# Three flags in place of one for the weights' low parts in a macaron transformer block

## The chip, the cores and the metric

The kernel runs on one core of a Trainium2 chip. The metric is the device time of one execution in microseconds, from the first instruction to the last with what lies around them; smaller is better. TensorE is called PE here, VectorE DVE, ScalarE ACT, GpSimd POOL and the engine that issues the transfers SP.

## The reference

The input is x of 16 x 256 tokens with 128 features. Three residual steps follow one another: half a feed-forward network, a 16-head self-attention, and the same half feed-forward network again.

```python
x = x + 0.5 * ffn(layernorm(x));  x = x + attention(layernorm(x));  x = x + 0.5 * ffn(layernorm(x))

def ffn(x):                                   # weights -1, 0 or 1, with a scale per output
    h = silu(tlin(x, w1, s1)) * tlin(x, w2, s2)      # 128 -> 512, twice
    h = gelu(tlin(h, h1, sh1)); h = gelu(tlin(h, h2, sh2))   # 512 -> 512
    return tlin(h, w3, s3)                            # 512 -> 128
```

Everything is float32.

## The kernel before, in words

A float32 product is made of matmuls in a shorter format. Every operand is split into a high part (a copy in that format) and a low part (what is left of it). `split_mm` (line 939) multiplies high weights by the high and the low part of the data. With `general` true it adds the low weights times both parts, which doubles the matmuls. If every low part of the weights is zero, these products add nothing, and the shorter form is exact.

The weights come as eleven chunks of 128 x 512 in seven groups (`W_GROUPS`): group 0 is w1, group 1 is w2, groups 2, 3 and 4 up to chunk 6 hold h1 and the start of h2 (group 2 is one chunk, groups 3 to 6 two each), and groups 5 and 6 hold the rest of h2 and w3. ACT makes the high part of a group (`weight_hi`, line 444), DVE the low parts of groups 0 and 1 (`weight_lo`, line 624), POOL those of groups 2 to 6 (line 387). DVE reduces the low part of each group to its largest magnitude (`weight_lo_max`, line 629), then the seven of them to one (`all_lo_max`), a matmul with a column of ones sums this over the partitions, DVE copies the sum into `flag`, and PE loads the flag into a register (line 1182). `If_ne` on the register (line 1183) then chooses between two written-out versions of the rest of the phase, `ffn_bodies` with `general` true or false. The register also chooses the version in the second feed-forward phase.

The tokens are taken in blocks of 512, two blocks to a pass. A pass is `layer1` (eight tiles t; each a product with w1, the gate, and one with w2, the up), then `hidden` four times (h1 for block 0 and 1, then h2 for block 0 and 1; four tiles of eight matmuls each), and `output`. The first `layer1`, before the flag is known, always takes the general form: 64 matmuls in place of 32. Inside a tile of `layer1`, ACT applies silu and DVE multiplies it by the up product (`silu<-bank,S,silu`); ACT then makes the high part of the result and DVE its low part (`act_lo<-silu,act_hi`). In `hidden`, ACT applies gelu twice and DVE makes the low part (`act_lo<-full,act_hi`).

Nothing plans the order: each engine has its own written list, and semaphores join them. The functions take `between` tables that put extra work behind a tile. PE's list is the one of the functions under `block.tensor`. The gate product of tile t waits for the silu of tile t-3, and the up product for DVE's product of tile t-3. A wait on PE holds all that stands behind it.

Of the kernel before, what the change touches and what calls it, by code (L numbers as in the profile page):

```python
# [56 lines left out]
W_GROUPS = ((0, 1), (1, 2), (2, 3), (3, 5), (5, 7), (7, 9), (9, 11))  # L57
W_RAW = 3


def macaron_kernel(nc, x, w_ffn, w_att, s12, sg, s3, bqk, bv, bo, eye, sel, low_rows, out):
# [11 lines left out]
    with ctx:  # L73
# [31 lines left out]
        newton = sb("newton", [P, 8])  # L105
        lo_max = sb("lo_max", [P, len(W_GROUPS) + 1])
        flag = sb("flag", [1, 1])
        xn = sb("xn", [P, 8, P])
# [330 lines left out]
        def _(act):  # L439
# [61 lines left out]
            def ffn_phase(f):  # L501
# [32 lines left out]
                if f == 0:  # L534
                    weight_hi(0)
                    weight_hi(1)
                    split_x(nb, 0)
                    weight_hi(2)
                    split_x(nb + 1, 1)
                    weight_hi(3)  # L540
                    act.wait_ge(consts_in, 16 * N_CONSTS)
                    layer1(t1, {t: lambda k=t + 4: weight_hi(k) for t in range(3)})
                    act.wait_ge(s3_half, 1)
                else:
                    layer1(t1, {3: lambda: o_to_sbuf(NBATCH - 1)})
# [73 lines left out]
        def _(dve):  # L619
# [16 lines left out]

            def all_lo_max():
# [5 lines left out]
            def take_flag():  # L643
                dve.wait_ge(flag_sum, 1)
                D.tensor_copy(flag[:, :], bank[6][0:1, 0:1]).then_inc(flag_set, 1)

# [143 lines left out]
            def ffn_phase(f):  # L790
                t1, t2, nb, n0 = f * NB * HT, f * NP * HID_TILES, f * NB, f * NORMS1

                def body(i, first=False, more=True):
# [8 lines left out]
                    for step in steps[0:1]:  # L802
                        step()

                    def first_step():
# [35 lines left out]
                if f == 0:  # L841
# [13 lines left out]
                    side = {t: lambda k=t + 2: weight_lo_max(k) for t in range(5)}  # L855
                    layer1(t1, side | {5: all_lo_max, 6: take_flag})

# [77 lines left out]
        def _(pe):  # L935
# [155 lines left out]
            def ffn_bodies(f, general):  # L1091
                t1, t2, nb, nx = f * NB * HT, f * NP * HID_TILES, f * NB, f * XN1

                def body(i, first=False, more=True):
# [3 lines left out]
                    pe.wait_ge(h_full, hl + 6)  # L1098
                    hidden(g, 0, 0, h_lo, hl + HT, general)
                    before = nb + 2 * i - 2  # L1100
# [11 lines left out]
                    hidden(g + HT, 0, 1, h_lo, hl + 2 * HT, general, back | ({3: tokens} if into_att else {}))  # L1112
                    hidden(g + 2 * HT, 1, 0, g_lo, g + HT + SLOTS, general,
# [38 lines left out]
                if f == 1:  # L1152
# [6 lines left out]
                    pe.wait_ge(att_added, NBATCH)  # L1159
                body(0, first=True)  # L1160
                with pe.Fori(1, NP - 1) as i:
# [3 lines left out]
            def ffn_phase(f, low_weights):  # L1165
                if f == 0:
                    pe.wait_ge(eye_in, 16)
                    transpose_x(0, 0)
                    transpose_x(1, 1)

                    pe.wait_ge(w_lo, 2)
                    def sum_low_max():


                        pe.wait_ge(ones_set, 1)
                        pe.wait_ge(lo_reduced, len(W_GROUPS) + 1)
                        MM(bank[6][0:1, 0:1], ONES[:, 0:1], lo_max[:, len(W_GROUPS):len(W_GROUPS) + 1],
                           start=True, stop=True).then_inc(flag_sum, 1)
                    layer1(0, 0, True)
                    sum_low_max()  # L1180
                    pe.wait_ge(flag_set, 1)
                    pe.reg_load(low_weights, flag[0:1, 0:1].bitcast(I32))
# [143 lines left out]
```

## Time and profile before

| | us |
|---|---|
| median of three runs | 709.23 |
| lowest and highest of them | 693.59, 713.70 |
| the profiled execution: its time, its span | 703.42, 701.6 |
| PE busy in the span | 665.2 (95%) |
| DVE, ACT, POOL busy | 459.1, 470.3, 72.4 |

Times in the rows count from the start of the span. A row of the timeline has the start, the duration, the engine, the line, the operation, what it writes and reads, and, in brackets, how long the engine sat idle before it and what ended that. The granted clock of PE (PEclk) is 1.00 at its upper level of 2.4 GHz and 0.50 at 1.2 GHz. What concerns the change lies in the first 60 us of the span.

### The profile page before, as it was taken

The numbers are of one execution on the slowest core, as the hardware profiler recorded it, in microseconds if no ns is written. First come the engines' busy times: TensorE is split into PE (matmuls) and PEld (weight loads), VectorE is DVE, ScalarE is ACT, GpSimd is POOL, SyncE is SP. The second block draws the span as 40 slices with busy tenths as digits, with TensorE's granted clock in tenths as the row PEclk, the third lists the DMA queues.
The fourth block names the chain that finished last, engine by engine and source line by source line (L and its number), as shares of the span: only waits on it lengthen the run. The fifth ranks groups of instructions, "written<-read, shape, count | busy, mean of one in ns | idle before, by whom it ended". The sixth has DMA issues, their size and how long they took to land.

```text
span 701.6 us, 13215 instructions
## 1 busy us (share of the span) xinstructions
PE 665.2 (95%) x4514; PEld 486.0 (69%) x4514; DVE 459.1 (65%) x1067; ACT 470.3 (67%) x786; POOL 72.4 (10%) x240
## 2 busy tenths in 40 slices
PE   2869999999998999999999999999989999999997
PEld 1658888888775656666666666666557887888885
DVE  4845756658548658787878787777218575675742
ACT  2747878879652447676767676766467787886974
POOL 3501010100100102020202020002000101010000
PEclk9989999999995569999999999999589999999999
DMA  8200000000063333242424242400000000100001
GB/s 269 68 2 1 0 1 1 0 0 0 1 240 121 121 116 126 106 137 104 140 100 140 100 139 98 144 1 2 0 3 2 0 1 1 31 1 30 0 30 31
DMA packets 37361, 42.22 MB, mean 60 GB/s; under 512 B 2624, under 2 KB 27968, under 8 KB 37312
## 3 DMA queue, kind: packets, MB, share of 16 engines
q1 hardware_dynamic: 37312, 41.57, 17.4%
q8 instruction: 31, 0.51, 0.3%
q14 instruction: 18, 0.15, 0.1%
HBM read 22.69 MB, written 18.87 MB: 59 GB/s over the span
## 4 chain that ended last, share of the span: by engine, by line
PE 67%; issue 22%; DVE 4%; POOL 3%; ACT 3%; DMA 1%; POOLq 0%; ACTq 0%
PE bank L947 22%; PE bank L1056 11%; PE bank L1031 11%; PE bank L1043 6%; PE bank L1045 5%; PE bank L1074 3%; PE bank L1016 1%; PE bank L1012 1%; PE bank L1088 1%; PE bank L1020 1%; DVE neg_max L758 1%; POOL WL L389 1%; PE bank L1081 1%; POOL newton L366 1%; PE bank L994 1%
## 5 line engine op out<-in xcount | busy, mean ns | idle before, releaser
L947 PE MATMUL bank<-act_hi,WH 128*128 128x512 f32 x576 | 229.3, 398 | 8.0 <-issue 5.1
L947 PE MATMUL bank<-act_lo,WH 128*128 128x512 f32 x576 | 225.3, 391 | 0.0
L758 DVE TENSOR_REDUCE neg_max<-bank 128x2 f32<-128x512 f32 x256 | 169.6, 684 | 61.6 <-PE bank L1031 60.6
L557 ACT ACTIVATE probs<-bank 128x512 f32<-128x512 f32 x256 | 144.6, 597 | 91.7 <-PE bank L1045 90.5
L717 DVE TENSOR_TENSOR act_lo<-full,act_hi 128x512 fp32r<-128x512 f32 x128 | 87.8, 688 | 114.1 <-ACT act_hi L479 113.9
L1043 PE MATMUL bank<-QA,KA 32*128 32x256 f32 x512 | 134.2, 348 | 0.1
L947 PEld LDWEIGHTS bank<-act_hi,WH 128*128 128x128 f32 x576 | 108.7, 189 | 35.0 <-issue 6.4
L477 ACT ACTIVATE full<-bank,SG 128x512 f32<-128x512 f32 x128 | 88.2, 689 | 62.4 <-PE bank L947 62.3
L947 PEld LDWEIGHTS bank<-act_lo,WH 128*128 128x128 f32 x576 | 108.8, 189 | 22.3 <-issue 0.5
L1045 PE MATMUL bank<-m_parts,SEL 32*128 32x256 f32 x512 | 114.2, 290 | 0.0
L1031 PEld LDWEIGHTS bank<-KA,QA 32*128 32x128 f32 x512 | 61.8, 199 | 66.7 <-DVE neg_max L758 46.3
L1031 PE MATMUL bank<-KA,QA 32*128 32x256 f32 x512 | 99.6, 349 | 2.2 <-DVE neg_max L758 1.9
L1043 PEld LDWEIGHTS bank<-QA,KA 32*128 32x128 f32 x512 | 86.2, 197 | 8.3 <-ACT probs L557 5.3
L1056 PE MATMUL bank<-probs,V 128*32 128x256 f32 x1024 | 87.6, 416 | 0.1
L1045 PEld LDWEIGHTS bank<-m_parts,SEL 32*128 32x128 f32 x512 | 87.6, 201 | 0.0
L479 ACT ACTIVATE act_hi<-bank,SG 128x512 fp32r<-128x512 f32 x128 | 87.2, 681 | 0.0
L706 DVE SCALAR_TENSOR_TENSOR silu<-bank,S,silu 128x512 f32<-128x512 f32 x64 | 47.0, 743 | 17.9 <-ACT silu L464 10.5
L947 PE MATMUL bank<-x_hi,WH 128*128 128x512 f32 x128 | 51.9, 406 | 3.7 <-issue 2.9
L947 PE MATMUL bank<-x_lo,WH 128*128 128x512 f32 x128 | 51.3, 401 | 0.0
L464 ACT ACTIVATE silu<-bank,S 128x512 f32<-128x512 f32 x64 | 43.0, 682 | 8.6 <-PE bank L947 8.5
L697 DVE TENSOR_TENSOR act_lo<-silu,act_hi 128x512 fp32r<-128x512 f32 x64 | 45.7, 714 | 0.2
L456 ACT ACTIVATE act_hi<-silu 128x512 fp32r<-128x512 f32 x64 | 40.2, 628 | 6.7 <-DVE silu L706 6.6
(82 smaller groups left out, 571.5 us busy)
## 6 DMA issues: line engine op xcount, KB each, us to landing
qk_scratch<-qk SPq DMA_DIRECT2D x64, 256.0 KB, 2.6
QA<-qk_scratch SPq DMA_DIRECT2D x16, 512.0 KB, 3.8
KA<-qk_scratch SPq DMA_DIRECT2D x16, 512.0 KB, 5.3
X<-x SPq DMA_DIRECT2D x4, 512.0 KB, 9.6
raw_rest<-w_ffn SPq DMA_DIRECT2D x4, 512.0 KB, 6.3
out<-X SPq DMA_DIRECT2D x4, 512.0 KB, 3.2
raw<-w_ffn SPq DMA_DIRECT2D x3, 256.0 KB, 4.3
WA<-w_att SPq DMA_DIRECT2D x1, 256.0 KB, 5.0
```

The costliest lines, as they stand in the source:

```text
L477: A.activation(full[:, t, :], bank[4 + t % 2][:, :], ACT.Gelu, scale=SG[:, layer, t:t + 1])
L479: A.activation(act_hi[1 + layer][:, j, t, :], bank[4 + t % 2][:, :], ACT.Gelu, scale=SG[:, layer, t:t + 1]).then_inc(g_hi, 1)
L557: A.activation(probs[:, v % 8, :], bank[2 + v % 2][:, :], ACT.Exp, scale=SCALE)\
L697: D.tensor_tensor(act_lo[0][:, t // HT, t % HT, :], silu[:, t % SLOTS, :], act_hi[0][:, t // HT, t % HT, :].bitcast(F32), op=ALU.subtract)\
L706: D.scalar_tensor_tensor(out=silu[:, t % SLOTS, :], in0=bank[UP_BANKS[t]][:, :], scalar=S12[:, 1, t % HT:t % HT + 1], in1=silu[:, t % SLOT ...
L717: D.tensor_tensor(act_lo[1 + layer][:, j, t, :], full[:, t, :], act_hi[1 + layer][:, j, t, :].bitcast(F32), op=ALU.subtract)\
L758: D.tensor_reduce(neg_max[:, bb, qt, n0:n0 + 2], bank[A_BANKS[u]][:, :].rearrange("p (h k) -> p h k", h=2), axis=AX.X, op=ALU.max, negate= ...
L947: ins = MM(dst, a, b, start=k == 0, stop=k == len(todo) - 1)
L1031: ins = MM(bank[A_BANKS[u]][:, SEQ * i:SEQ * i + SEQ], QA[rows, 2 * par + bb, 2 * jj + i, P * qt:P * qt + P], KA[rows, 2 * par + bb, 2 * j ...
L1043: MM(dst, KA[rows, 2 * par + bb, 2 * jj + i, P * kt:P * kt + P], QA[rows, 2 * par + bb, 2 * jj + i, :], start=True, stop=False)
L1045: ins = MM(dst, SEL[rows, 2 * jj + i, :], m_parts[rows, bb, :], start=False, stop=True)
L1056: ins = MM(bank[4][32 * h:32 * h + 32, SEQ * (g % 2):SEQ * (g % 2) + SEQ], V[par][:, 2 * bb + kt, col:col + 32], probs[:, (4 * g + 2 * kt ...
```

## The change

Three flags are made instead of one, each over some of the groups: flag 0 over groups 0 and 1 (w1, w2), flag 1 over groups 2 to 4, and flag 2 over all seven. Flag 0 is loaded before anything else on PE, and an `If_ne` on it encloses the transposes of x and the first `layer1`, which now has a general and a short version. Flag 1 is summed behind tile 4 and loaded behind tile 6 of that `layer1`, and an `If_ne` on it encloses the first two calls of `hidden`. Flag 2 is summed inside the second of these calls, behind its tile 2, and loaded behind it; the `If_ne` on it encloses the rest, as the only one did before. ACT converts groups 0 to 4 before it splits x, in place of groups 0 and 1, with 2 and 3 between the halves. DVE reduces groups 0 and 1 and makes flag 0 before it normalises x, reduces group 2 behind that, groups 3 and 4 in `layer1`, and groups 5 and 6 in the second call of `hidden`.

```diff
+FLAGS = ((0, 2), (2, 5), (0, 7))
...
@@ scalar
-                    weight_hi(0)
-                    weight_hi(1)
+                    for k in range(5):
+                        weight_hi(k)
                     split_x(nb, 0)
-                    weight_hi(2)
                     split_x(nb + 1, 1)
-                    weight_hi(3)
                     act.wait_ge(consts_in, 16 * N_CONSTS)
-                    layer1(t1, {t: lambda k=t + 4: weight_hi(k) for t in range(3)})
+                    layer1(t1, {t: lambda k=t + 5: weight_hi(k) for t in range(2)})
                     act.wait_ge(s3_half, 1)
+                    act.wait_ge(w_lo_rest, len(W_GROUPS) - 2)
...
@@ vector
+            def flag_lo_max(f):
                 G = len(W_GROUPS)
-                dve.wait_ge(lo_reduced, G)
-                D.tensor_reduce(lo_max[:, G:G + 1], lo_max[:, 0:G], axis=AX.X, op=ALU.max)\
+                a, b = FLAGS[f]
+                dve.wait_ge(lo_reduced, b + f)
+                D.tensor_reduce(lo_max[:, G + f:G + f + 1], lo_max[:, a:b], axis=AX.X, op=ALU.max)\
                     .then_inc(lo_reduced, 1)
...
+                        third = (lambda: weight_lo_max(5), lambda: weight_lo_max(6), last_flag)
...
-                        hidden(g + HT, 0, 1)
+                        hidden(g + HT, 0, 1, third)
...
                     weight_lo(0)
                     weight_lo(1)
+                    weight_lo_max(0)
+                    weight_lo_max(1)
+                    flag_lo_max(0)
+                    take_flag(0)
                     normalise(n0, 0, 0)
                     normalise(n0, 4, 4)
+                    weight_lo_max(2)
                     low_x(nb, 0)
-                    weight_lo_max(0)
-                    weight_lo_max(1)
                     low_x(nb + 1, 1)
...
-                    layer1(t1, side | {5: all_lo_max, 6: take_flag})
+                    layer1(t1, {1: lambda: weight_lo_max(3), 2: second_flag, 5: lambda: take_flag(1)})
...
@@ tensor
+                        layer1(0, 0, general, {4: second_sum, 6: lambda: load_flag(1)})
+                    def first_hidden(general):
+                        pe.wait_ge(h_full, 6)
+                        hidden(0, 0, 0, h_lo, HT, general)
+                        hidden(HT, 0, 1, h_lo, 2 * HT, general, {2: lambda: sum_low_max(2)})
+                    pe.wait_ge(ones_set, 1)
+                    sum_low_max(0)
+                    load_flag(0)
+                    with pe.If_ne(low_weights, 0):
+                        first_layer1(True)
+                    with pe.Else():
+                        first_layer1(False)
+                    with pe.If_ne(low_weights, 0):
+                        first_hidden(True)
+                    with pe.Else():
+                        first_hidden(False)
+                    load_flag(2)
```

PE, the start of its list in the changed kernel (1188 is the line of the flag's sum, 1009 the transposes of x, 962 the matmuls of `split_mm`). The branch leads to the short version, 71 rows further down, whose first rows stand behind the dots:

```order
L1188 MATMUL bank<-lo_max,ONES 1x1 [waits lo_reduced,ones_set]
L1193 TENSOR_LOAD flag [waits flag_set]
L1213 COMPARE_AND_BRANCH
L1009 MATMUL bank<-EYE,xn 128x128 [waits xn_done,eye_in]
...
L1213 UNCONDITIONAL_BRANCH
L1009 MATMUL bank<-EYE,xn 128x128 [waits xn_done,eye_in]
L1009 MATMUL bank<-EYE,xn 128x128 x3
```

The transposes of x, first in the list before, now stand behind a flag and a branch.

PE in the changed kernel, from the load of flag 1 to the branch on it, and from the sum of flag 2 to the branch on it (both in the short versions):

```order
L1193 TENSOR_LOAD flag [waits flag_set]
L962 MATMUL bank<-x_hi,WH 128x512 [waits silu_done]
...
L962 MATMUL bank<-x_hi,WH 128x512 [waits h_full]
...
L1217 COMPARE_AND_BRANCH
...
L1188 MATMUL bank<-lo_max,ONES 1x1 [waits lo_reduced]
L962 MATMUL bank<-act_hi,WH 128x512 [waits g_hi]
...
L1193 TENSOR_LOAD flag [waits flag_set]
L1222 COMPARE_AND_BRANCH
```

Between the load of flag 1 and its branch stand the four matmuls of tile 7; between the sum of flag 2 and its load the eight of the last tile of `hidden`.

DVE from the low parts of groups 0 and 1 on, in the kernel before and then in the changed one:

```order
L626 TENSOR_TENSOR WL<-raw,WH 128x512 [waits w_hi] x2
L685 TENSOR_SCALAR xn<-X,moments,rstd 128x128 [waits rstd_done]
...
L691 TENSOR_TENSOR x_lo<-bank,x_hi 128x512 [waits xhi_done]
L634 TENSOR_REDUCE lo_max<-WL 128x1 [waits w_lo] x2
L691 TENSOR_TENSOR x_lo<-bank,x_hi 128x512 [waits xhi_done]
```

```order
L626 TENSOR_TENSOR WL<-raw,WH 128x512 [waits w_hi] x2
L634 TENSOR_REDUCE lo_max<-WL 128x1 [waits w_lo] x2
L642 TENSOR_REDUCE lo_max<-lo_max 128x1 [waits lo_reduced]
L647 COPY flag<-bank 1x1 [waits flag_sum]
L687 TENSOR_SCALAR xn<-X,moments,rstd 128x128 [waits rstd_done]
...
L634 TENSOR_REDUCE lo_max<-WL 128x1 [waits w_lo_rest]
L693 TENSOR_TENSOR x_lo<-bank,x_hi 128x512 [waits xhi_done] x2
```

The two reductions and the flag now stand ahead of the normalisation, and a reduction that waits for POOL stands ahead of the low part of x.

## Rows read from the trace of the kernel before

**Rows 1.** Waits of PE over the whole span: total us, times, longest us

```profile
PE bank L947 <- issue: 8.0, 2, 5.1
```

**Rows 2.** Timeline of PE and DVE, from the last matmul of the first layer1

```profile
32.16 0.40 PE L947 MATMUL bank<-x_lo,WL 128*128 128x512 f32 x1
...
34.22 0.15 DVE L640 TENSOR_REDUCE lo_max<-lo_max 128x1 f32<-128x7 f32 x1
...
34.51 0.19 PE L1177 MATMUL bank<-lo_max,ONES 128*1 128x1 f32 x2 [1.95 <-DVE lo_max L640]
...
35.55 0.14 DVE L645 COPY flag<-bank 1x1 f32<-1x1 f32 x1
...
39.77 0.77 PE L947 MATMUL bank<-act_hi,WH 128*128 128x512 f32 x1 [5.07 <-issue]
```

**Rows 3.** PE's sequencer by line: flag load, If, loop's branch; ns min/median/max, first and last start

```profile
L1182 PEldq TENSOR_LOAD <-flag x1: 489/489/489, 35.7 to 35.7; - x1
...
L1183 PEldq COMPARE_BRANCH  x2: 3327/3346/3365, 36.3 to 518.9; - x2
...
L1161 PEldq COMPARE_BRANCH  x4: 76/153/236, 123.6 to 658.8; - x4
```

**Rows 4.** Stretches: length, busy us (count) of PE, PEld, DVE, ACT, POOL; PEclk, DMA

```profile
39.80:42.80 3.00, 3.00 (x7) 2.43 (x8) 0.00 (x0) 0.00 (x0) 0.00 (x0) 0.50 0.02 5
...
522.50:527.50 5.00, 5.00 (x16) 4.12 (x17) 1.01 (x2) 1.89 (x3) 0.00 (x0) 0.50 0.01 3
```

**Rows 5.** Timeline of all engines, the start

```profile
7.78 1.29 DVE L626 TENSOR_TENSOR WL<-raw,WH 128x512 fp32r<-128x512 f32 x2
...
11.95 2.13 DVE L685 TENSOR_SCALAR xn<-X,moments,rstd 128x128 f32<-128x128 f32 x8 [2.88 <-POOL rstd L372]
...
13.21 2.05 PE L994 MATMUL bank<-EYE,xn 128*128 128x128 f32 x8 [13.21 <-DVE xn L685]
...
14.96 0.69 DVE L691 TENSOR_TENSOR x_lo<-bank,x_hi 128x512 fp32r<-128x512 f32 x1 [0.88 <-ACT x_hi L451]
...
15.52 1.28 POOL L389 TENSOR_TENSOR WL<-raw,WH 128x512 fp32r<-128x512 f32 x1 [3.61 <-ACT WH L446]
15.57 1.27 DVE L634 TENSOR_REDUCE lo_max<-WL 128x1 f32<-128x512 f32 x2
...
15.80 0.76 PE L947 MATMUL bank<-x_hi,WH 128*128 128x512 f32 x1 [0.54 <-DVE x_lo L691]
```

**Rows 6.** The weights' transfers, by line: ns, first and last issue us

```profile
L280 SPq DMA_DIRECT2D raw_rest<-w_ffn x4: 432/432/433, 4.7 to 6.1; - x4
...
DMA to landing us min/median/max: 4.2/5.1/7.5
```

**Rows 7.** Timeline of DVE and ACT in the first layer1

```profile
19.81 1.05 ACT L446 ACTIVATE WH<-raw_rest 128x1024 fp32r<-128x1024 f32 x1
...
21.46 0.75 DVE L706 SCALAR_TENSOR_TENSOR silu<-bank,S,silu 128x512 f32<-128x512 f32 x1 [0.18 <-ACT silu L464]
22.13 1.76 DVE L697 TENSOR_TENSOR act_lo<-silu,act_hi 128x512 fp32r<-128x512 f32 x1
...
28.42 1.10 DVE L697 TENSOR_TENSOR act_lo<-silu,act_hi 128x512 fp32r<-128x512 f32 x1
...
31.83 1.20 DVE L634 TENSOR_REDUCE lo_max<-WL 128x1 f32<-128x1024 f32 x1
...
33.62 0.68 DVE L697 TENSOR_TENSOR act_lo<-silu,act_hi 128x512 fp32r<-128x512 f32 x1
```

**Rows 8.** Timeline of PE and DVE, end of the second call of hidden

```profile
55.17 0.39 PE L947 MATMUL bank<-act_hi,WH 128*128 128x512 f32 x1
...
56.67 0.69 DVE L717 TENSOR_TENSOR act_lo<-full,act_hi 128x512 fp32r<-128x512 f32 x1 [1.12 <-ACT act_hi L479]
...
56.98 0.39 PE L947 MATMUL bank<-act_hi,WH 128*128 128x512 f32 x1
```

**Rows 9.** All instructions on the low weights, whole span: ns, first and last start

```profile
L947 PE MATMUL bank<-x_hi,WL x16: 389/389/628, 16.8 to 31.9; 128*128 128x512 f32 x16
```

More of the change, by code:

```diff
@@ L105, in macaron_kernel @@
         newton = sb("newton", [P, 8])
-        lo_max = sb("lo_max", [P, len(W_GROUPS) + 1])
-        flag = sb("flag", [1, 1])
+        lo_max = sb("lo_max", [P, len(W_GROUPS) + len(FLAGS)])
+        flag = sb("flag", [1, len(FLAGS)])
         xn = sb("xn", [P, 8, P])
@@ L635, in weight_lo_max, with take_flag @@
                                 apply_absolute_value=True).then_inc(lo_reduced, 1)
-            def all_lo_max():
+            def flag_lo_max(f):
                 G = len(W_GROUPS)
-                dve.wait_ge(lo_reduced, G)
-                D.tensor_reduce(lo_max[:, G:G + 1], lo_max[:, 0:G], axis=AX.X, op=ALU.max)\
+                a, b = FLAGS[f]
+                dve.wait_ge(lo_reduced, b + f)
+                D.tensor_reduce(lo_max[:, G + f:G + f + 1], lo_max[:, a:b], axis=AX.X, op=ALU.max)\
                     .then_inc(lo_reduced, 1)
-            def take_flag():
-                dve.wait_ge(flag_sum, 1)
-                D.tensor_copy(flag[:, :], bank[6][0:1, 0:1]).then_inc(flag_set, 1)
+            def take_flag(f):
+                dve.wait_ge(flag_sum, f + 1)
+                D.tensor_copy(flag[:, f:f + 1], bank[6][0:1, 0:1]).then_inc(flag_set, 1)
             def norm_steps(n, tile0, width=8, biased=0):
@@ L803, in body, with last_flag @@
                         step()
+                    third = ()
+                    if f == 0 and first:
+                        def last_flag():
+                            flag_lo_max(2)
+                            take_flag(2)
+                        third = (lambda: weight_lo_max(5), lambda: weight_lo_max(6), last_flag)
                     def first_step():
@@ L854, in ffn_phase, with second_flag @@
                     D.tensor_scalar(S3H[:, :], S3[:, :], 0.5, None, ALU.mult).then_inc(s3_half, 1)
-                    side = {t: lambda k=t + 2: weight_lo_max(k) for t in range(5)}
-                    layer1(t1, side | {5: all_lo_max, 6: take_flag})
+                    def second_flag():
+                        weight_lo_max(4)
+                        flag_lo_max(1)
+                    layer1(t1, {1: lambda: weight_lo_max(3), 2: second_flag, 5: lambda: take_flag(1)})
                     dve.wait_ge(max_cleared, 1)
@@ L1092, in ffn_bodies, with body @@
                 t1, t2, nb, nx = f * NB * HT, f * NP * HID_TILES, f * NB, f * XN1
-                def body(i, first=False, more=True):
+                def body(i, first=False, more=True, begun=False):
                     g = t2 + HID_TILES * i
@@ L1097, in body @@
                     into_att = f == 0 and not more
-                    pe.wait_ge(h_full, hl + 6)
-                    hidden(g, 0, 0, h_lo, hl + HT, general)
+                    if not begun:
+                        pe.wait_ge(h_full, hl + 6)
+                        hidden(g, 0, 0, h_lo, hl + HT, general)
                     before = nb + 2 * i - 2
@@ L1111, in values @@
                         project_v(0)
-                    hidden(g + HT, 0, 1, h_lo, hl + 2 * HT, general, back | ({3: tokens} if into_att else {}))
+                    if not begun:
+                        hidden(g + HT, 0, 1, h_lo, hl + 2 * HT, general, back | ({3: tokens} if into_att else {}))
                     hidden(g + 2 * HT, 1, 0, g_lo, g + HT + SLOTS, general,
@@ L1159, in ffn_bodies @@
                     pe.wait_ge(att_added, NBATCH)
-                body(0, first=True)
+                body(0, first=True, begun=f == 0)
                 with pe.Fori(1, NP - 1) as i:
@@ L1166, in ffn_phase @@
                 if f == 0:
[L1167 to L1177, printed above, removed]
-                           start=True, stop=True).then_inc(flag_sum, 1)
@@ L1179, in ffn_phase, with sum_low_max, load_flag @@
[L1179 to L1182, printed above, removed]
+                    def sum_low_max(k):
+                        pe.wait_ge(lo_reduced, FLAGS[k][1] + k + 1)
+                        MM(bank[6][0:1, 0:1], ONES[:, 0:1], lo_max[:, len(W_GROUPS) + k:len(W_GROUPS) + k + 1],
+                           start=True, stop=True).then_inc(flag_sum, 1)
+                    def load_flag(k):
+                        pe.wait_ge(flag_set, k + 1)
+                        pe.reg_load(low_weights, flag[0:1, k:k + 1].bitcast(I32))
@@ new lines, in first_layer1, with second_sum @@
+                    def first_layer1(general):
+                        pe.wait_ge(eye_in, 16)
+                        transpose_x(0, 0)
+                        transpose_x(1, 1)
+                        def second_sum():
+                            pe.wait_ge(xlo_done, 1)
+                            sum_low_max(1)
+                        layer1(0, 0, general, {4: second_sum, 6: lambda: load_flag(1)})
[3 more added lines that the diff above has]
+                        hidden(HT, 0, 1, h_lo, 2 * HT, general, {2: lambda: sum_low_max(2)})
```

## The prediction

> **What bounds the kernel now.** I began with the page: PE is busy for 95% of the span, so a change helps by shortening PE's waits or removing its matmuls. The waits of PE [rows 1] name the largest that no other engine's work explains, 5.1 us. The timeline puts it at the flag [rows 2]: PE's last matmul of the first layer1 ends at 32.6 and the first of hidden starts at 39.77. Four things follow one another in this gap: DVE's seven reductions to one (34.22, 0.15 us), the sum (34.51), the copy, which stands behind other DVE work (35.55), and the load and branch. The sequencer's rows price the last two [rows 3]: a load 0.49 us, an `If` 3.33 us, and 3.37 us in the second phase, where no load precedes it. The stretches [rows 4] show an aftermath: the granted clock of PE is 0.50 when work resumes, and seven matmuls start in 3.0 us, one each 0.43 us. At the upper level eight start in 1.81 us (55.17 to 56.98), one each 0.23 us [rows 8].
>
> The 64 matmuls of the first layer1 are not its only limit. DVE's list there [rows 7] has, for most tiles, a product (0.73), a low part (0.68 alone; 1.10 to 1.76 while POOL subtracts) and a reduction (1.20). So halving the matmuls gives less than 32 times 0.23 us: the next limit is DVE.
>
> The low parts are all zero: the low weights appear in 16 matmuls each with x_hi and x_lo, the last by 32.2, and nowhere afterwards [rows 9], so each `If` led to the short form. The three new ones will too.
>
> **The change, part by part.**
>
> *The start.* DVE has made the low parts of w1 and w2 by 9.07 [rows 5]. Two reductions (1.27 us) and the small one (0.15, with 0.05 for its wait) bring it to 10.54, and the sum starts 0.14 later, as at 34.51 [rows 2]. From that sum's start to the copy's the trace has 1.04 us, but DVE was busy with other work; between its 0.19 us and 1.04 I take 0.35, since nothing else delays the copy here. Copy (0.14), load (0.04 and 0.49) and a near branch (0.24) end at about 12.0, with the upper bound at 12.7. The transposes start at 13.21 because they wait for xn. The cost is nothing; that cover is about a microsecond.
>
> For the price of a near `If` the trace has two sorts of rows [rows 3]: the far `If` at 3.33 us and the loop's branch, 0.24 us back over the body. The first new branch passes 71 rows of PE's list and the second 130, fewer than a loop's body; the far one passes over a thousand. By distance the nearest row is the loop's, and I take 0.24, with 3.35 as the other end. The Trainium skill ("Runtime: NRT & Kernel Launch", Instruction fetch mechanics) says that a taken branch stalls for a fetch if its target is outside the window of two blocks of 256 instructions. By that the first two would be cheap and the third dear, which is the sum below; no run here shows a near `If`.
>
> *ACT's five conversions ahead of x.* The last transfer concerned is the second of the four; issued at 4.7 and 0.43, it lands within 7.5 us, by 12.7 at the latest and by 10.3 at the median [rows 6]. A conversion of two chunks takes 1.05 us [rows 7]. ACT's next work is due when half of the transposes (2.05 us from 13.21) [rows 5] are through, at about 14.2. Nothing is lost.
>
> *POOL's subtractions ahead of time.* POOL is free at 11.9 and will work through the normalisation (2.13 us on DVE, from 11.95). DVE's operations under a subtraction give two rows: low parts with two inputs in SBUF slow down to 1.10 or 1.76 [rows 7]; the two reductions, with one, take their 1.27 beside POOL's 1.28 [rows 5]. The normalisation has one such input, so I take no cost. The reduction of group 2 (0.67) then fits before 14.96, where DVE waited 0.88 us.
>
> *Layer 1.* DVE's first product starts about 0.86 us earlier, since the first gate has two matmuls fewer at 0.43. The reduction of group 2, gone from behind it, gives nothing, because the second product waited for ACT anyway (0.18 us at 21.46), where a conversion (19.81) stands ahead of its silu, before and now. Two reductions of 1.20 move out and a small one (0.2) comes in. The low part that started at 33.62 then starts at 30.6, and the copy of flag 1, which stands behind it, at 31.2. Load: done at 31.9. The four matmuls of tile 7 stand behind that load. Before them, behind tile 4, PE waits for the sum of flag 1, some 5 us by the same count along DVE's list. DVE is the slower of the two there, so nobody is late for it, but I expect the clock at its lower level: 4 times 0.43 is 1.7, and the near branch lies beneath them. **Hidden starts at 33.6 in place of 39.77: 6.2 us gained.** From there to the second call of hidden I keep the old pace.
>
> *The sum of flag 2.* In old times, the last tile of the second hidden starts at 55.17. Now PE first waits for DVE to end the low part of tile 2 (56.67 and 0.69), the small reduction (0.15) and the handover (0.14), then sums (0.19): 57.75 at the earliest. **2.6 us lost.** The reductions of groups 5 and 6 nearly fit the 1.12 us in which DVE waits [rows 8].
>
> *The load and the third branch.* PE's sequencer reaches the load about 0.4 us into the last tile (eight matmuls, 1.81 us). Load and far branch (0.49, 3.35, and 0.25 of handovers) end 4.5 us into it. **2.6 us lost**, up to 3.2 if the copy needs the whole 1.04.
>
> *The clock after that.* Two gaps of over 2 us stand there. After the gap of 2.9 us in the second phase the clock was 0.50 from 522.5 to 527.5 [rows 4]. Seven matmuls 0.2 us slower: **1.4 us lost**, between nothing and that.
>
> Sum: -6.2 + 2.6 + 2.6 + 1.4 = +0.4 us on 703.42. All later work is unchanged and on PE, which carries the shift to the end.
>
> **The rivals.** *Each `If` costs 3.35 us however near (slower).* For it: both `If` rows of the trace do, and loops come back to rows that have run. Then the first branch ends at about 15.1, and the transposes start near 15.3 instead of 13.21: 2.1. The second starts at 32.1 and ends at 35.5, 1.9 late. Sum +4.4. It decides from a near branch of about 1.5 us upwards at the start.
>
> *The clock holds (faster).* For it: no new gap is as long as the 7.2 us of before. Tile 7 gains 0.8, the start of hidden 1.4, and the loss of 1.4 is gone: -3.2. Against it: the gap of 2.9 us.
>
> *POOL slows the normalisation.* If xn is stretched as the low parts were, by 1.10/0.68 or 1.76/0.68, it takes 3.4 to 5.5 instead of 2.13; 0.2 of that is covered: +1.1 to +3.2 on the start, the sum +1.5 to +3.6. The Trainium skill ("GPSIMD Engine Reference", Key points) says that POOL contends with DVE instructions of two SBUF inputs or in a two-port mode. The trace agrees for the two inputs (1.76); for xn no run here shows it.
>
> *A flag isn't zero, so that the short form isn't taken at once.* Then the gain falls away and the 5.2 of flag 2 stay. Against it: the sum over all groups led to the short form [rows 9].
>
> **How the numbers follow.** Forecast 0.50, dear branches 0.18, the clock holds 0.17, POOL 0.13, a flag 0.02. They lie between -3.2 and +6.6 us, all under 1%, so "no change" stands in every one. What can be told from no change is about 2%, 14 us, which the runs shown span by themselves: 693.59 to 713.70, with the profiled execution at 703.42 and the median, 709.23, 5.8 above it. So I set the forecast on the middle of these four times, 706.3, and add 0.4: 707 us. For 8 in 10 I take the scatter of the runs and the cases: 694 to 717. Faster by over 2%: 0.09, within 2%: 0.85, slower: 0.06; the shares outside come from the scatter, with the median of before on its upper side.
>
> **What would show it.** The first branch's row reads 0.1 to 0.3 us and the transposes still start at 13.2; the first matmul of hidden starts at 33 to 34; PE then has two gaps of 2 to 2.6 us around the last tile of the second hidden, and the third call starts near 56.0, in place of 56.98. It is wrong if the first branch reads 3.3, if xn takes over 2.5 us, if DVE doesn't hold the copy of flag 1 until about 31, or if the time moves by more than 10 us, since nothing here is worth that.

## The result, and the profile after

| | before | after |
|---|---|---|
| median of 20 runs each, us | 709.5 | 713.77 |
| ratio after/before, 95% interval | | 1.0193 [1.0156, 1.023] |
| profiled execution: time, span, mean granted clock | 703.42, 701.6, 0.946 | 713.95, 711.9, 0.948 |
| at mean clock 0.95, us | 702.3 | 711.4 (+9.05 ± 0.60) |

The kernel became slower, where no change was forecast: by 0.6% in the medians, by 1.9% in the ratio and by 1.3% at equal clock. The ratio and its interval rest on the quickest runs of each kernel, and so on the clock that those happened to get. The last row takes the clock out, and needs a word. The 57 runs of before that were taken beside the experiments go from 692 us at a clock of 0.968 to 722 at 0.915, and in the profiled executions the stretches in which the clock is 0.50 differ in length. The longest begin in the attention, as in this row of the page of the changed kernel (40 slices of 17.8 us, tenths of full speed):

```profile
PEclk9999999999997569999999999599989999999999
```

Slices 13 to 15 (7, 5 and 6) lie in the attention, whose instructions the change doesn't touch. So I fitted one straight line through the 176 runs whose clock is on record, 20 of after and all those of the experiments with before beside them (the 20 of before in the table, one of them at 1188 us, have no clock on record): one slope for all, -533 us per unit of mean granted clock, and a level for each kernel; the runs scatter about it by 1.2 us. "At equal clock" below is the difference of these levels, with its 95% half-width. It would miss a clock that the change itself lowers; the means, 0.945 over the runs of after and 0.941 over those of before, show none. The ratios of the plain times stand beside it.

The waits of PE in the changed kernel (total us, times, longest us):

```profile
PE bank L1188 <- DVE lo_max L642: 17.3, 3, 10.9
PE bank L1009 <- DVE xn L687: 7.4, 1, 7.4
PE bank L962 <- issue: 4.2, 2, 2.9
PE bank L962 <- DVE act_lo L719: 2.7, 3, 2.2
```

Against [rows 1], the stall of 5.1 us named "issue" is gone. What is left of that name stands in the second phase: the 2.9 us at the far branch, as before, and 1.33 us behind the third matmul after it, which are new (in before, 5.1 and 2.9 make up the 8.0):

```profile
527.90 0.69 PE L962 MATMUL bank<-x_hi,WH 128*128 128x512 f32 x1 [2.90 <-issue]
...
530.78 0.79 PE L962 MATMUL bank<-x_lo,WH 128*128 128x512 f32 x1 [1.33 <-issue]
```

The sums of the three flags (L1188) wait instead; 10.9 us of that is the start, where PE had nothing to do. PE's sequencer, by line (ns min/median/max, first and last start), answers [rows 3]:

```profile
L1193 PEldq TENSOR_LOAD <-flag x3: 308/311/489, 11.3 to 54.6; - x3
...
L1213 PEldq COMPARE_BRANCH  x1: 223/223/223, 11.9 to 11.9; - x1
...
L1217 PEldq COMPARE_BRANCH  x1: 350/350/350, 36.7 to 36.7; - x1
...
L1222 PEldq COMPARE_BRANCH  x2: 3352/3417/3482, 55.0 to 524.4; - x2
```

The near branches cost 0.22 and 0.35 us, the far ones 3.4. The start (timeline of all engines), against [rows 5]:

```profile
10.90 0.19 PE L1188 MATMUL bank<-lo_max,ONES 128*1 128x1 f32 x2 [10.90 <-DVE lo_max L642]
...
11.13 0.15 DVE L647 COPY flag<-bank 1x1 f32<-1x1 f32 x1 [0.37 <-PE bank L1188]
...
12.20 1.26 POOL L390 TENSOR_TENSOR WL<-raw,WH 128x512 fp32r<-128x512 f32 x1
12.28 7.14 DVE L687 TENSOR_SCALAR xn<-X,moments,rstd 128x128 f32<-128x128 f32 x8 [1.00 <-POOL rstd L373]
13.42 4.64 POOL L390 TENSOR_TENSOR WL<-raw_rest,WH 128x1024 fp32r<-128x1024 f32 x2
...
18.54 2.05 PE L1009 MATMUL bank<-EYE,xn 128*128 128x128 f32 x8 [7.45 <-DVE xn L687]
...
21.04 0.79 PE L962 MATMUL bank<-x_hi,WH 128*128 128x512 f32 x1 [0.45 <-DVE x_lo L693]
```

The eight normalising operations took 2.13 us before and 7.14 now, in the same stretch as POOL's three subtractions (12.20 to 18.06). Taken apart (timeline of DVE, in narrow windows), three of them have all of the loss:

```profile
12.28 1.26 DVE L687 TENSOR_SCALAR xn<-X,moments,rstd 128x128 f32<-128x128 f32 x1 [1.00 <-POOL rstd L373]
13.46 2.38 DVE L687 TENSOR_SCALAR xn<-X,moments,rstd 128x128 f32<-128x128 f32 x1
15.76 2.38 DVE L687 TENSOR_SCALAR xn<-X,moments,rstd 128x128 f32<-128x128 f32 x1
18.06 1.36 DVE L687 TENSOR_SCALAR xn<-X,moments,rstd 128x128 f32<-128x128 f32 x5
```

Each of the three ends 0.08 us after one of the subtractions (13.46, 15.76 and 18.06), and the other five keep the old pace. The transposes start 5.3 us later. Flag 1 (timeline of PE and DVE; matmuls of tiles 5, 6 and 7 behind the sum), against [rows 2, 7]:

```profile
32.53 0.19 PE L1188 MATMUL bank<-lo_max,ONES 128*1 128x1 f32 x2 [4.24 <-DVE lo_max L642]
...
36.09 0.14 DVE L647 COPY flag<-bank 1x1 f32<-1x1 f32 x1
...
36.64 0.47 PE L962 MATMUL bank<-x_hi,WH 128*128 128x512 f32 x1 [0.54 <-DVE flag L647]
...
37.64 0.40 PE L962 MATMUL bank<-act_hi,WH 128*128 128x512 f32 x1
```

Three stretches of the same kernel (length, busy us and count of PE, PEld, DVE, ACT, POOL, then PEclk), against [rows 4]:

```profile
33.00:36.50 3.50, 3.10 (x8) 1.89 (x6) 3.50 (x8) 3.04 (x5) 0.00 (x0) 0.51 0.01 2
36.60:41.00 4.40, 4.36 (x19) 3.57 (x20) 3.85 (x12) 2.38 (x3) 0.00 (x0) 1.00 0.01 4
...
58.60:63.00 4.40, 4.38 (x19) 3.58 (x20) 2.62 (x9) 1.65 (x3) 0.00 (x0) 1.00 0.01 4
```

The clock drops behind the wait of 4.24 us, but for tiles 5 and 6, and is back at its upper level for tile 7 and hidden. Flag 2, and the third call of hidden (timeline of PE and DVE), against [rows 8]:

```profile
54.19 0.19 PE L1188 MATMUL bank<-lo_max,ONES 128*1 128x1 f32 x2 [2.15 <-DVE lo_max L642]
54.31 0.50 PE L962 MATMUL bank<-act_hi,WH 128*128 128x512 f32 x1
...
54.42 0.15 DVE L647 COPY flag<-bank 1x1 f32<-1x1 f32 x1 [0.28 <-PE bank L1188]
...
58.62 0.47 PE L962 MATMUL bank<-act_hi,WH 128*128 128x512 f32 x1 [2.19 <-DVE act_lo L719]
...
61.49 0.39 PE L962 MATMUL bank<-act_hi,WH 128*128 128x512 f32 x1
...
65.22 0.39 PE L962 MATMUL bank<-act_hi,WH 128*128 128x512 f32 x1
```

Up to 58.62 the changed kernel is only 1.64 us late (56.98 before). The two last rows show where most of the rest went. Between them lie 16 matmuls of the unchanged part: 3.73 us, 0.233 each, at a full clock. Before it was 0.227: 55.17 to 56.98 are eight [rows 8]. Taken over 560 to 680 us, starts of successive matmuls on the weights lie 227.4 ns apart before and 233.3 after (480 and 472 distances, those above 0.3 us left out). The trace has 1,408 such matmuls in the short form: 1,408 times 5.9 ns are 8.3 us, of which waits may hide a part.

### The profile page after: what moved, and what is told of

The parts are those of the page before. It is cut to its first block, busy times and chain, and to the rows that moved or that the text cites. A ratio compares the mean times of both kernels' runs of the same rounds, so it can differ in the third digit from the quotient of the medians.

```text
span 711.9 us, 13168 instructions
## 1 busy us (share of the span) xinstructions
PE 667.7 (94%) x4486; PEld 480.3 (67%) x4486; DVE 464.7 (65%) x1071; ACT 471.3 (66%) x786; POOL 72.5 (10%) x240
## 4 chain that ended last, share of the span: by engine, by line
PE 67%; issue 21%; DVE 5%; POOL 3%; DMA 2%; ACT 1%; SPq 0%; POOLq 0%; ACTq 0%
PE bank L962 23%; PE bank L1071 11%; PE bank L1046 10%; PE bank L1058 6%; PE bank L1060 5%; PE bank L1089 3%; PE bank L1027 1%; DVE neg_max L760 1%; PE bank L1103 1%; PE bank L1035 1%; PE bank L1031 1%; DVE xn L687 1%; DMA KA<-qk_scratch 1%; PE bank L1096 1%; PE bank L1022 1%
## 5 line engine op out<-in xcount | busy, mean ns | idle before, releaser
L962 PE MATMUL bank<-act_hi,WH 128*128 128x512 f32 x576 | 231.7, 402 | 3.9 <-DVE act_lo L719 2.7
L962 PE MATMUL bank<-x_hi,WH 128*128 128x512 f32 x128 | 54.4, 425 | 3.9 <-issue 2.9
L962 PE MATMUL bank<-x_lo,WH 128*128 128x512 f32 x128 | 53.7, 419 | 1.3 <-issue 1.3
```

Of the source, the lines that this page charges most:

```text
L962: ins = MM(dst, a, b, start=k == 0, stop=k == len(todo) - 1)
```

## Two theories, and how they were told apart

**The addresses** (theory A in the expectations). `lo_max` has ten columns now in place of eight. In the compiled programs' addresses it takes 64 bytes of a partition in place of 32, and all tiles declared behind it, among them x_hi, x_lo and the act tiles, which hold the data that goes through the matmuls, lie 32 bytes further on (x_hi at byte 94112 instead of 94080). The weights, declared ahead of it, stay. If that sets the pace, the loss behind 58.62 isn't the flags' doing. **POOL** (theory D). The subtractions that ACT's early conversions release run beside the normalisation and stretch it. The other explanations weighed against these (of the code's place, the order of the work, the clock) stand in the quoted expectations.

All results; "pace" is the distance of matmul starts from 560 to 680 us, "third" the start of the third call of hidden:

| kernel | median us (runs) | ratio to before, 95% | equal clock, us | pace ns | xn us | third us |
|---|---|---|---|---|---|---|
| before | | 1 | 0 | 227.4 | 2.13 | 56.98 |
| after | 713.77 (20) | 1.0193 [1.0156, 1.023] | +9.05 ± 0.60 | 233.3 | 7.14 | 58.62 |
| e1 before, data tiles +32 B | 710.41 (6) | 1.0173 [1.0053, 1.0293] | +6.6 ± 1.0 | 233.3 | 2.14 | |
| e2 after, data tiles +64 B | 713.21 (6) | 1.0195 [1.0086, 1.0303] | +5.5 ± 1.0 | 228.9 | 7.16 | |
| e3 after, POOL held back | 710.75 (6) | 1.0197 [1.0108, 1.0287] | +3.4 ± 1.0 | 233.3 | 2.14 | 54.06 |
| e4 before, early conversions | 711.06 (12) | 1.0073 [0.9977, 1.0169] | +5.5 ± 0.7 | 227.1 | 7.14 | |
| e5 after, data tiles +128 B | 714.71 (6) | 1.026 [1.0134, 1.0386] | +7.6 ± 1.0 | 232.4 | 7.14 | 59.36 |
| e6 e5 and POOL held back | 710.78 (6) | 1.0127 [0.9921, 1.0333] | +1.8 ± 1.0 | 232.6 | 2.14 | 53.46 |
| e7 e6 and flag 2 earlier | 705.08 (6) | 1.0142 [1.0048, 1.0236] | +0.6 ± 1.0 | 232.6 | 2.14 | 51.29 |
| e8 e7 and the second phase's branch turned | 696.15 (6) | 0.9995 [0.9873, 1.0116] | -3.0 ± 1.0 | 232.7 | 2.14 | 50.68 |
| e9 before, weights +32 B | 721.69 (14) | 0.9977 [0.9917, 1.0036] | +7.2 ± 0.7 | 233.3 | 2.14 | |
| e10 after, weights +32 B | 708.12 (13) | 1.0007 [0.9955, 1.0059] | +2.6 ± 0.7 | 227.3 | 7.15 | 58.63 |
| e11 after, all addresses kept | 710.7 (12) | 1.0074 [1.0009, 1.0139] | +3.7 ± 0.7 | 227.3 | 7.14 | 58.72 |
| e12 all mended | 697.52 (6) | none | -8.8 ± 1.0 | 227.3 | 2.14 | 50.38 |

The medians of before beside them were 705.99 (e1 to e4), 709.74 (e5 to e8) and 705.28 (e9 to e12). The difference of two levels of this table has an uncertainty of 0.8 to 1.3. e9's ratio and its level at equal clock disagree because the quickest three of its runs had clocks of 0.960 to 0.968 and the other eleven 0.920 to 0.945; the pace is read where the clock is at its upper level and doesn't depend on it.

## The experiments on the addresses

**e1: the kernel before, with nothing changed but the place of the data tiles.**

```diff
         flag = sb("flag", [1, 1])
+        pad = sb("pad", [1, 1])
         xn = sb("xn", [P, 8, P])
```

> The kernel before with 32 unused bytes behind the flag, so that every tile behind it, the operands act_hi, act_lo, x_hi and x_lo that the matmuls stream among them, starts 32 bytes further on, as in the changed kernel (at 32 beyond a multiple of 64 in place of at the multiple). Theory A (the address of the streamed operand sets the rate): the 128x512 matmuls start every 233 ns in place of 227, in both feed-forward phases; 1408 of them times 6 ns make the kernel slower by about 8.5 us; the first hidden still starts near 39.8. Rival B (the rate belongs to the execution or the chip): 227 ns or a mixture, and the same time. Rival C (the rate comes from the changed program's code and branches): 227 ns, the same time.

An unused tile of 32 bytes costs 6.6 us, of 8.5 expected, and gives the pace of the changed kernel. Two rows, 16 matmuls apart, from PE's timeline (3.73 us, 0.233 each):

```profile
59.73 0.39 PE L948 MATMUL bank<-act_lo,WH 128*128 128x512 f32 x1
...
63.46 0.39 PE L948 MATMUL bank<-act_lo,WH 128*128 128x512 f32 x1
```

The first call of hidden starts at 39.89 (39.77 in before) and xn is at 2.14, so nothing of the front moved. Theory A holds, and no flag or branch is needed for this part.

**e2: the changed kernel, the data tiles moved by 64 bytes in place of 32.**

```diff
         flag = sb("flag", [1, len(FLAGS)])
+        pad = sb("pad", [1, 1])
```

> The changed kernel with 32 unused bytes behind the flags, so that all tiles behind them start at a multiple of 64 bytes again. Theory A: a matmul every 227 ns, about 8.5 us faster than the changed kernel, so within 1 to 3 us of the kernel before; the start is unchanged (normalisation about 7.1 us, first matmul of layer1 near 21). Rivals B and C: 233 ns or a mixture, no gain.

The pace comes back nearly (228.9 ns) and 3.6 ± 1.1 us of time with it, not the 8.5 expected. By the pace (4.4 of 5.9 ns) some 4.9 of e1's 6.6 ± 1.0 would be due; the two uncertainties cover the difference.

**e5: by 128 bytes.**

```diff
         flag = sb("flag", [1, len(FLAGS)])
+        pad = sb("pad", [1, 24])
```

> The changed kernel with 96 unused bytes behind the flags: the tiles behind them start 128 bytes further on than in the kernel before, so at multiples of 128 as there (the version moved by 64 had 229 ns a matmul, the kernel before 227). Theory A2 (what counts is the start modulo 128): 227 ns, and at the same granted clock 6 to 7 us faster than the changed kernel, so about 2 us slower than before, which is what the start costs (the first h2 product 1.6 us late). Rival (modulo 64 counts, and the 229 ns has another cause in the changed program): 229 ns.

A miss: 232.4 ns. That the start modulo 128 bytes decides is refuted, since the data tiles stand there as in the kernel before. What stayed possible was their absolute place, or their place relative to the weights.

**e9 and e10: the weights moved instead, in the kernel before and in the changed one.** S12, a tile of 32 bytes, is declared ahead of the weights.

```diff
         X = sb("X", [P, NT, P])
+        S12 = sb("S12", [P, 2, HT])
         WH = sb("WH", [P, W_CHUNKS, 512], F32R)
         WL = sb("WL", [P, W_CHUNKS, 512], F32R)
         WA = sb("WA", [P, 4, P])
-        S12 = sb("S12", [P, 2, HT])
```

> The kernel before, with the small tile S12 declared ahead of the converted weights, so that the weights' high parts lie 32 bytes further on and the streamed tiles (x_hi, act_hi and the others) stay where they were. Theory R (the place of the stationary weights relative to the streamed tile sets the pace): the relation is broken as it was by the change, so a 128x512 matmul starts every 233 ns in both feed-forward phases, and the time is about 6.5 us above before at the same granted clock. Theory S (only the place of the streamed tile counts): 227 ns as in the kernel before, and no change of time within 1.5 us. Start and hidden as before under both: xn 2.1 us, first matmul of hidden near 39.8.

> The changed kernel with the same move, so that weights and streamed tiles both lie 32 bytes further on than in the kernel before and stand to each other as they did there. Theory R: 227 ns again, and 6 to 7 us less than the changed kernel, which leaves about 2.5 us above before at the same clock. Theory S: 233 ns, and the time of the changed kernel, about 9 us above before. xn stays at 7.1 us and the third call of hidden near 58.6 minus what the pace returns, under both.

In e9 the data tiles stand where they stood, and the pace is lost (16 matmuls in 3.73 us), with 7.2 us of time:

```profile
59.67 0.40 PE L947 MATMUL bank<-act_lo,WH 128*128 128x512 f32 x1
...
63.40 0.40 PE L947 MATMUL bank<-act_lo,WH 128*128 128x512 f32 x1
```

In e10 both stand 32 bytes further on, and it is back (eight in 1.82 us), with 6.4 us less than the changed kernel:

```profile
65.11 0.39 PE L962 MATMUL bank<-act_lo,WH 128*128 128x512 f32 x1
...
66.92 0.39 PE L962 MATMUL bank<-act_lo,WH 128*128 128x512 f32 x1
```

So it is the place of the streamed data relative to the weights (theory R). PE loads the next weights while it streams (PEld is busy beside PE in every stretch above), and the two reads could get in each other's way; that is a guess, which no run here shows. Which distances are slow isn't settled by these: as in before 227.4, +32 bytes 233.3, +64 228.9, +128 232.4, and -32 (e9) 233.3.

**e11: the changed kernel with every data tile and weight at its old address.**

```diff
-        scrap = sb("scrap", [P, 1])
...
-        lo_max = sb("lo_max", [P, len(W_GROUPS) + len(FLAGS)])
+        lo_max = sb("lo_max", [P, len(W_GROUPS) + len(FLAGS) + 1])
+        scrap = lo_max[:, len(W_GROUPS) + len(FLAGS):]
```

> The changed kernel with the scratch column put into the last column of lo_max, so that no streamed tile and no weight has another place than in the kernel before. Theory A (the changed kernel lost its pace through the addresses alone): 227 ns in both phases, and what is left of the loss is the start's: the third call of hidden near 58 in place of 56.98, and 1 to 3 us above before at the same clock. If something else in the change slowed the matmuls, they stay at 233 ns and the time at 9 us above before.

227.3 ns, and 5.4 us less than the changed kernel. What the flags and the order of the work cost by themselves is 3.7 us here, a little over the 1 to 3 expected, and 2.6 in e10. Of this 1.7 have come about by the third call of hidden (58.72). The rest, 2.0 and 0.9 with 0.7 either way, is about the size of the second stall in the second phase: PE stops there for 1.54 us in e11 and 1.71 in e10. That stall stands in every kernel with three flags whose branch in the second phase is far (after, e2, e3, e5, e6, e7, e10 and e11: 1.2 to 2.1 us) and in none of before, e1, e4 and e9. What PE waits for there the profile doesn't name, and no run takes it away by itself.

## The experiments on the start and on the flags

**e4: the kernel before, with ACT's early conversions alone.**

```diff
-                    weight_hi(0)
-                    weight_hi(1)
+                    for k in range(5):
+                        weight_hi(k)
                     split_x(nb, 0)
-                    weight_hi(2)
                     split_x(nb + 1, 1)
-                    weight_hi(3)
                     act.wait_ge(consts_in, 16 * N_CONSTS)
-                    layer1(t1, {t: lambda k=t + 4: weight_hi(k) for t in range(3)})
+                    layer1(t1, {t: lambda k=t + 5: weight_hi(k) for t in range(2)})
```

> The kernel before with one part of the change alone: ACT converts five weight groups ahead of x, so POOL's subtractions begin at about 12 us; one flag as before, tiles where they were. Theory D: the normalisation takes about 7 us and the first matmul of layer1 starts near 20.8 in place of 15.8; some of the 5 us comes back since POOL is done earlier, so 3 to 5 us slower than before at 227 ns a matmul. Rival E: the normalisation stays at 2.1 us and the time is the same as before.

The start of e4 (timeline of DVE and POOL):

```profile
12.07 1.26 POOL L389 TENSOR_TENSOR WL<-raw,WH 128x512 fp32r<-128x512 f32 x1
12.15 7.14 DVE L683 TENSOR_SCALAR xn<-X,moments,rstd 128x128 f32<-128x128 f32 x8 [2.90 <-POOL rstd L372]
13.29 4.64 POOL L389 TENSOR_TENSOR WL<-raw_rest,WH 128x1024 fp32r<-128x1024 f32 x2
```

The same 7.14 us without any flag, and 5.5 us at the end. None of it came back, where some was expected to: the first hidden starts at 45.00, 5.2 later than before. So the early conversions do it; that it is POOL's subtractions, and not the conversions themselves, e3 shows.

**e3: the changed kernel, POOL's subtractions held back until x is normalised.**

```diff
             rsqrt_steps(0, 0)
+            pool.wait_ge(xn_done, 2)
             for k in range(2, len(W_GROUPS)):
...
                     normalise(n0, 4, 4)
-                    weight_lo_max(2)
                     low_x(nb, 0)
                     low_x(nb + 1, 1)
+                    weight_lo_max(2)
```

> The changed kernel, but POOL waits with its subtractions until x is normalised, and DVE's reduction of group 2 stands behind the low parts of x. Theory D (POOL's subtractions stretch the normalisation): the eight normalising instructions take 2.1 us in place of 7.1, the first matmul of layer1 starts near 16 in place of 21, the first hidden near 33 in place of 37.6; 4 to 5 us faster than the changed kernel, and still slower than before by the matmuls' rate (233 ns). Rival E (something else stretches it, the transfers of the start or ACT's conversions): it stays near 7 us.

The start of e3 (timeline of DVE, POOL and PE), with the copy of flag 1:

```profile
11.98 2.14 DVE L688 TENSOR_SCALAR xn<-X,moments,rstd 128x128 f32<-128x128 f32 x8 [0.98 <-POOL rstd L373]
...
14.20 1.27 POOL L391 TENSOR_TENSOR WL<-raw,WH 128x512 fp32r<-128x512 f32 x1 [2.25 <-DVE xn L688]
...
15.74 0.79 PE L963 MATMUL bank<-x_hi,WH 128*128 128x512 f32 x1 [0.45 <-DVE x_lo L694]
...
30.83 0.14 DVE L648 COPY flag<-bank 1x1 f32<-1x1 f32 x1
```

xn is back at 2.14, with ACT's conversions as early as in the changed kernel, and layer1 starts as in the kernel before. Theory D holds. 5.7 ± 1.1 us at equal clock come back, the third call of hidden starts at 54.06, 2.9 earlier than before, and what stays is the pace (233.3 ns). The ratio, 1.0197, doesn't show it: its runs had low clocks.

**e6: both, on e5's addresses** (the edits of e5 and e3 together).

> As the run moved by 128 bytes, and POOL's subtractions wait until x is normalised. If the two causes add, the normalisation takes 2.1 us, a matmul 227 ns, and the time at the same clock is 5 to 6 us under that run and 2 to 4 us under the kernel before. If they overlap (the late subtractions hold up DVE's low parts and the flags), the gain over that run is 2 us or less.

5.8 us less than e5 at equal clock: the gain of e3 again. The pace on e5's addresses stays at 232.6 ns, so the time is 1.8 us above before, and not 2 to 4 below.

**e7: flag 2 earlier as well.** Groups 5 and 6 are reduced ahead of the first hidden, the sum stands behind tile 3 of the first call, and the copy at tile 0 of the second.

```diff
-                        third = (lambda: weight_lo_max(5), lambda: weight_lo_max(6), last_flag)
+                        weight_lo_max(5)
+                        weight_lo_max(6)
+                        flag_lo_max(2)
+                        third = (lambda: take_flag(2),)
...
-                        hidden(0, 0, 0, h_lo, HT, general)
-                        hidden(HT, 0, 1, h_lo, 2 * HT, general, {2: lambda: sum_low_max(2)})
+                        hidden(0, 0, 0, h_lo, HT, general, {3: lambda: sum_low_max(2)})
+                        hidden(HT, 0, 1, h_lo, 2 * HT, general)
```

> As the run before it, with groups 5 and 6 reduced ahead of the first hidden, flag 2 summed on PE behind tile 3 of the first hidden and copied behind the first low part of the second: PE no longer stops for DVE inside the second hidden. If that stop (2.15 us) is on the path, the time falls by about 2 us; the far branch behind the second hidden (2.2 to 2.5 us of waiting) stays. If the reductions hold up the low parts of the first hidden instead, nothing is gained.

The third call starts 2.2 us earlier than in e6, PE's stop for the sum of flag 2 is gone, and the time at equal clock falls by 1.2 ± 1.3, which isn't clear of nothing.

**e8: the branch of the second phase asks for zero first,** so that the short version stands next to it.

```diff
+                if f == 1:
+                    with pe.If_eq(low_weights, 0):
+                        ffn_bodies(f, False)
+                    with pe.Else():
+                        ffn_bodies(f, True)
+                    return
```

> As the run before it, and in the second feed-forward phase alone the condition is turned round, so that the short version follows the branch and the general one is jumped over at the end. If a branch costs a fetch only where it is taken to a far place, the 2.9 us between the attention and that phase go (the branch reads 0.1 us), the jump at the end hides behind the last transfers, and the time falls by 2 to 4 us with the clock's loss after the gap. If any If costs 3.3 us, nothing changes.

3.7 ± 1.3 us less than e7. PE's sequencer at the new branch in e8:

```profile
L1225 PEldq COMPARE_BRANCH  x2: 83/1856/3628, 512.7 to 688.2; - x2
```

Asked at 512.7 it takes 83 ns, and the second stall, 1.18 us in e7, is gone with the first (3.39). The far jump, over the general version, starts at 688.2, with PE's last matmuls (in e12 at 674.2), and ends at 691.8, before the span does (693.4).

**e12: all of it, on the old addresses** (the edits of e11, e3, e7 and e8).

> The changed kernel with the addresses of before, POOL's subtractions held back until x is normalised, flag 2 summed behind tile 3 of the first hidden and copied in the second, and the branch of the second phase turned so that the short version is the near one. If the parts add up (addresses -6.6, held subtractions about -5, early third flag about -1 to -2, turned branch -3.7 us against the changed kernel): 8 to 10 us below the kernel before at the same clock, 227 ns, xn 2.1 us, third call of hidden near 51 and no wait named issue on PE in the second phase. If the parts share one gain, it is 3 to 6 us below.

PE's waits in e12 have no row named issue. Its four first rows:

```profile
PE bank L1189 <- DVE lo_max L643: 15.0, 2, 10.7
PE bank L963 <- ACT act_hi L481: 3.6, 8, 1.6
PE bank L1047 <- DVE neg_max L761: 2.5, 6, 0.7
PE bank L1010 <- DVE xn L688: 2.4, 1, 2.4
```

-8.8 ± 1.0 us at equal clock, in the range given for parts that add up; against the changed kernel it is 17.9 ± 1.1, where the parts measured one by one (5.4, 5.7, 1.2 and 3.7) make 16.0. The medians are 697.52 and 705.28 (0.989), the quickest runs 681.57 and 693.32 (0.983); the runs of the two overlap. At equal clock it beats both kernels.

## Why the prediction was wrong, step by step

Late (+) or early (-) against the kernel before, in the profiled executions, us:

| place | forecast | after |
|---|---|---|
| first matmul of layer1 (15.80 before) | 0 | +5.24 |
| first of hidden (39.77) | -6.2 | -2.13 |
| last tile of the second hidden (55.17) | -3.6 | -0.86 |
| third call of hidden (56.98) | -1.0 | +1.64 |
| the end, at equal clock | +0.4 | +9.05 |

The median, 713.77, lies in the range given, 694 to 717. That is luck: the range was made of the scatter of the runs, and of the loss of 9.05 us at equal clock the sum had foreseen 0.4.

**The step that failed most: "All later work is unchanged and on PE, which carries the shift to the end."** The instructions were unchanged; their pace was not, and in the second phase PE stops a second time (1.33 us). Moving the data tiles by 32 bytes cost 6.6 us without the flags (e1), and undoing it in the changed kernel gave back 5.4 (e11) to 6.4 (e10), where the sum had nothing. I had read what the order of the instructions showed, and not where the tiles lie. In the trace of before nothing could show it, but `lo_max` is declared with a column for every flag, and the addresses can be read from the compiled program.

**POOL's subtractions: "so I take no cost".** It cost 5.0 us on the start, and the sign given for it, xn over 2.5 us, came up. The rival that POOL slows the normalisation had 1.1 to 3.2, from the ratio 1.76/0.68 of one slowed operation [rows 7]. But the loss isn't a ratio. The three operations caught by a subtraction ended when it did, so the price is the length of POOL's instructions (1.26, 2.34 and 2.34), less what the three take alone. The trace of before had the same sign: the two slowed low parts of [rows 7] end at 23.89 and 29.52, each 0.55 us after one of these subtractions (timeline of POOL):

```profile
20.93 2.41 POOL L389 TENSOR_TENSOR WL<-raw_rest,WH 128x1024 fp32r<-128x1024 f32 x1 [1.62 <-ACT WH L446]
...
26.12 2.85 POOL L389 TENSOR_TENSOR WL<-raw_rest,WH 128x1024 fp32r<-128x1024 f32 x1
```

My reason for no cost, that the reductions of [rows 5] kept their pace beside POOL, holds for a reduction and not for this operation. The Trainium skill ("GPSIMD Engine Reference", Key points) says that POOL shares its SBUF interfaces with DVE and contends with instructions of two SBUF inputs or in a two-port mode; which of the two applies to the normalisation no run here shows, only that it was held up (after, e4) and not with POOL held back (e3).

**The gain at hidden, 6.2, was sound.** From the first matmul of layer1 to hidden it took 23.97 us before and 16.60 after, 7.4 less; with POOL held back (e3) the copy of flag 1 stood at 30.83, where "about 31" was forecast, and hidden started at 33.22, where 33.6 was.

**The clock: "1.4 lost".** It was not lost in this execution: the stretch from 58.60 has the clock at 1.00. It isn't sure to hold, either: in e10's profiled execution the clock was 0.66 on the mean of 58 to 63 us. And "I keep the old pace" after 33.6 missed a gain of the same kind, which only the rival of a clock that holds had, at 1.4: hidden started at a full clock, and its tile 2 came at 42.44 in place of 45.93, 1.4 more than the 2.1 at its start.

**What held.** The first flag was free (the copy starts 0.23 us after its sum, 0.35 forecast), the near branches cost 0.22 and 0.35 (0.24), PE's stop for the sum of flag 2 and the load with the far branch cost 2.6, of which some 0.2 are the slower pace, and 2.5 us (2.6 each, 2.7 if the terms are added exactly): from tile 2 at 42.44, 3.49 early, to the last tile, 0.86 early, and from there to the third call, 1.64 late. The rival of dear branches fell, and all flags were zero, as the short forms show. Through these steps alone the third call would have started near 56.0; the 5.24 of the start, less 1.2 and 1.4 gained in layer1 and hidden, make it 58.6.

## What to carry to other kernels

A diff that widens a small tile moves every tile declared behind it; where the time is made of thousands of equal matmuls, compare their distance before and after as the first thing, and keep new small tiles behind the large ones or in slack that is there. A conversion made early isn't free because its own engine is idle: look at what it releases, and beside whose work that will run. A branch belongs next to the version that is taken, and the far jump where PE has nothing left to do.

## What the runs showed of the hardware that was not expected

- 128x512 float32 matmuls start 227.4 or 233.3 ns apart at a full clock, depending on where the streamed data lie relative to the weights (e1, e9, e10), 2.6% of the pace. The Trainium skill ("SBUF — State Buffer", SBUF: two separate sides) says that within the engine side only the port pair shared by DVE and POOL causes contention, and that PE never waits on anyone. These runs don't show what PE loses the time to, but a pace that depends on two addresses is more than that rule gives.
- Eight normalising operations of 128x128 went from 2.13 to 7.14 us beside POOL's subtractions: three of them took as long as the subtraction that they met (1.26, 2.38 and 2.38 us), the other five 1.36 together. Two DVE reductions beside POOL kept 1.27 [rows 5].
- Over all runs the load of a flag into PE's register took 303 to 494 ns. A branch on it took 79 and 83 ns where the version wanted follows at once (e12, e8), 223 to 439 ns to one 71 or 130 rows on, and 3.3 to 3.8 us to a far one; in eight of the kernels a second stall of 1.2 to 2.1 us followed the far branch of the second phase, a few matmuls later.
